# A multi-scale convolution on one core: weights first in both load queues, and GpSimd's ring sum added last for every image

## The reference, cut to what matters

```python
# x (8, 32, 64, 64); _gn normalises each of the 32 channels of each image over its 64x64 pixels
def _L0_conv_ref(x, w1, w3, w5, w_proj):
    xd = jnp.concatenate([x[:, :, 0::2, 0::2], x[:, :, 0::2, 1::2],
                          x[:, :, 1::2, 0::2], x[:, :, 1::2, 1::2]], axis=1)   # 128 channels, 32x32
    feats = jnp.concatenate([_dwconv(xd, w1, 1), _dwconv(xd, w3, 3), _dwconv(xd, w5, 5)], axis=1)
    y = jnp.einsum('bchw,oc->bohw', feats, w_proj[:, :, 0, 0])                 # 384 -> 128 channels
    ll, lh, hl, hh = jnp.split(y, 4, axis=1)
    ...                                                                        # interleaved back to 64x64
    return out
x = x + _L0_conv_ref(_gn(x), L0_conv_w1, L0_conv_w3, L0_conv_w5, L0_conv_w_proj)
```

## Time and profile before

| what | value |
|---|---|
| median of 3 runs | 148.43 us (147.65 to 148.79) |
| the profiled execution: its own time | 149.9 us |
| its span, first to last instruction | 148.1 us |
| busy in the span: PE / DVE / ACT / POOL | 131.2 / 132.1 / 105.0 / 111.2 us |
| mean granted TensorE clock | 0.987 |

### The profile page before, as it was taken

One profiled execution on the slowest core, in us unless ns is written; L12 is line 12 of the kernel. 1 busy time (PEld: TensorE's weight loads), 2 busy tenths in 40 slices (PEclk: granted clock), 3 DMA queues, 4 the chain that ended last, 5 costly groups with the idle time before them and its releaser, 6 DMA issues.

```text
span 148.1 us, 1521 instructions
## 1 busy us (share of the span) xinstructions
PE 131.2 (89%) x505; PEld 97.7 (66%) x505; DVE 132.1 (89%) x147; ACT 105.0 (71%) x107; POOL 111.2 (75%) x81
## 2 busy tenths in 40 slices
PE   5789999699399999999999929999999999999470
PEld 5677787487276687767776616777777777687130
DVE  7559959999799998999999999999999999999651
ACT  2069943999999999989995999999999150050000
POOL 6138659779999999999999898989999997039000
PEclk9999999999999999999999999999999999999959
DMA  4999999201600700700525899152399927778333
GB/s 129 241 227 203 209 209 212 47 4 31 120 2 0 150 2 4 150 0 0 110 40 104 179 193 206 39 113 38 71 212 178 206 50 142 146 165 187 72 67 75
DMA packets 35799, 16.78 MB, mean 113 GB/s; under 512 B 34000, under 2 KB 34128, under 8 KB 35408
## 3 DMA queue, kind: packets, MB, share of 16 engines
q1 hardware_dynamic: 32720, 9.18, 31.9%
q0 software_dynamic: 1440, 7.04, 24.4%
q10 hardware_dynamic: 1632, 0.48, 1.4%
HBM read 5.46 MB, written 4.19 MB: 65 GB/s over the span
## 4 chain that ended last, share of the span: by engine, by line
DVE 55%; POOL 16%; PE 12%; DMA 7%; issue 5%; ACTq 1%; DVEq 1%; POOLq 0%
DVE ACC L595 38%; POOL RING_SUM L314 14%; DVE ACC L592 8%; PE YP L668 6%; DVE F L609 4%; DMA w_sb<-in_L_conv_w_dram 4%; DMA LO<-G 3%; PE YP L732 3%; PE YP L719 2%; POOL rstd L285 1%; DVE ACC L587 1%; DVE dev L519 1%; DVE F L605 1%; DVE ACC L599 1%; POOL LO L303 1%
## 5 line engine op out<-in xcount | busy, mean ns | idle before, releaser
L314 POOL TENSOR_TENSOR RING_SUM<-RING_SUM,PROD 128x900 f32<-128x900 f32 (+1 forms) x41 | 86.9, 2119 | 7.2 <-ACT PROD L434 3.4
L595 DVE SCALAR_TENSOR_TENSOR ACC<-G,coef,ACC 128x930 f32<-128x930 f32 (+1 forms) x63 | 75.3, 1195 | 2.0
L434 ACT ACTIVATE PROD<-G,coef 128x900 f32<-128x900 f32 (+1 forms) x41 | 40.8, 1055 | 0.0
L668 PE MATMUL YP<-LO,whi 128*128 128x512 f32 (+1 forms) x144 | 38.2, 417 | 2.3 <-DMA LO<-G 2.3
L668 PE MATMUL YP<-HI,wlo 128*128 128x512 f32 (+1 forms) x144 | 37.5, 413 | 0.0
L668 PE MATMUL YP<-HI,whi 128*128 128x512 f32 (+1 forms) x144 | 36.4, 407 | 0.3 <-DVE nbias L526 0.3
L668 PEld LDWEIGHTS YP<-LO,whi 128*128 128x128 f32 x144 | 27.3, 190 | 11.1 <-DMA LO<-G 2.7
L668 PEld LDWEIGHTS YP<-HI,whi 128*128 128x128 f32 x144 | 27.7, 194 | 7.8 <-issue 0.8
L668 PEld LDWEIGHTS YP<-HI,wlo 128*128 128x128 f32 x144 | 27.3, 190 | 8.5 <-issue 1.9
L417 ACT ACTIVATE Y<-YP 64x1024 f32<-64x1024 f32 x14 | 15.3, 1095 | 14.3 <-PE YP L719 14.1
L396 ACT ACTIVATE G<-X,nbias,rstd 64x1024 f32<-64x1024 f32 x16 | 21.0, 1312 | 4.8 <-DVE nbias L507 4.5
(11 more groups left out here) (63 smaller groups left out, 74.7 us busy)
## 6 DMA issues: line engine op xcount, KB each, us to landing
X<-in_x_dram SPq DMA_DIRECT2D x16, 256.0 KB, 5.4
LO<-G POOLq DMA_DIRECT2D x7, 543.0 KB, 4.7
X<-Y POOLq DMA_DIRECT2D x3, 1024.0 KB, 7.0
out_dram<-X SPq DMA_DIRECT2D x12, 256.0 KB, 4.7
out_dram<-X SPq DMA_DIRECT2D x6, 128.0 KB, 2.4
XS<-in_x_dram SPq DMA_DIRECT2D x2, 256.0 KB, 3.2
XS<-in_x_dram SPq DMA_DIRECT2D x1, 512.0 KB, 7.7
out_dram<-X ACTq DMA_DIRECT2D x2, 128.0 KB, 2.6
```

What stands on the lines that cost most here:

```text
L314: pool.tensor_tensor(dst, dst, prod(b, k), ALU.add).then_inc(prod_added, 1)
L434: act.activation(prod(b, k), g_tap(b, POOL_OF[b][k + 1]), ACT.Copy, scale=of5(POOL_OF[b][k + 1])).then_inc(prod_ready, 1)
L595: dve.scalar_tensor_tensor(part(ACC, tap), g_tap(b, tap), of5(tap), part(ACC, tap), ALU.mult, ALU.add).then_inc(acc_step, 1)
L668: mm = nc.tensor.matmul(dst, w[:, n, :], src, start=start, stop=False, skip_group_check=True)
```

## The change: weights first, and the ring sum last

Eight things are changed together.

1. Loads: SP issues `w5` and `w3` ahead of the `XS` loads; ACT issues the projection weights first, then `w1`, then the two halves of image 0, which SP had.
2. `LATE` holds all eight images: each begins with the scaled copy L587 and ends with the addition of `RING_SUM`.
3. `POOL_N` is 5, 6, 6, 6, 7, 7, 7, 8: 44 products on POOL in place of 41, and 76 DVE taps in place of 79. Image 0 has one DVE tap more, images 4 to 7 one less.
4. POOL issues `low_image(b+1)` after the third product of image b, not after its last. The third `add_x` stands after product 6 of image 7, the last one; before, after product 4, the last but one.
5. PE: `ring(3)` and `ring(4)` move behind the `high` sets of images 5 and 6 (before: behind the high-image-by-low-weights sets of images 4 and 5). Warm-up matmuls are 7 + 2 + 2 on the identity and 8 of 512 columns (before 9 and 10). PE's sum of the statistics of image 1 comes three taps earlier, and PE waits in image 2 for the variance of the last pairs, not for their bias.
6. The scaling of `weff` 6 to 8 goes from POOL to ACT. POOL waits for all three `whi` before its first `wlo`, and makes the spread of image 1's statistics after the first `wlo`.
7. DVE: the small statistics instructions with two SBUF tensors are written as `tensor_scalar` with a scalar read per partition; a copy of the mean is added. DVE permutes the projection weights before its two `part_bn` of image 0.
8. POOL's third `inv_std` stands one product earlier, DVE's `variance(2)` one tap earlier.

```diff
-POOL_TAPS = [(0, 2), (-2, -2), (-2, 2), (2, -2), (2, 2), (-2, -1), (2, 1)]
-POOL_N = [6, 6, 6, 6, 6, 6, 6, 7]
+POOL_TAPS = [(0, 2), (-2, -2), (-2, 2), (2, -2), (2, 2), (-2, -1), (2, 1), (-1, -2)]
+POOL_N = [5, 6, 6, 6, 7, 7, 7, 8]
-LATE = (0, 1, 7)
-ADD_X_AT = [(4, 2), (6, 2), (7, 4)]
+LATE = tuple(range(8))
+ADD_X_AT = [(4, 2), (6, 2), (7, 6)]
-WARM = (9, 10)
+WARM = (7, 2, 2, 8)
-RING_AFTER_HIGH = {2: 0, 3: 1, 4: 2, 7: 6}
+RING_AFTER_HIGH = {2: 0, 3: 1, 4: 2, 5: 3, 6: 4, 7: 6}
-RING_AFTER_WLO = {4: 3, 5: 4, 6: 5}
+RING_AFTER_WLO = {6: 5}
-INV_STD_AT = {(0, 3): (3, 2, 3), (1, 2): (4, 3, COLS)}
+INV_STD_AT = {(0, 2): (3, 2, 3), (1, 2): (4, 3, COLS)}
         def _(sp):
+            sp.dma_start(w_sb[:, 0:W3_AT], w5.rearrange("c a h w -> c (a h w)")).then_inc(w_loaded, 16)
+            sp.dma_start(w_sb[:, W3_AT:W1_AT], w3.rearrange("c a h w -> c (a h w)")).then_inc(w_loaded, 16)
             load_parts(sp, 0, 0, 512, xs_loaded[0])
             load_parts(sp, 0, 512, 1024, xs_loaded[1])
-            load_image(sp, 0, image_loaded[0])
             load_parts(sp, 1, 0, 1024, xs_loaded[2])
...
                 for k in range(N_PROD[b]):
+                    if k == NEXT_IMAGE_AT and b + 1 < B:
+                        low_image(b + 1)
                     pool.wait_ge(prod_ready, products_before(b) + k + 1)
...
-            for n in range(ACT_SCALED, N_INNER):
-                pool.tensor_scalar(weff[:, n, :], wpT[:, 2, :], of5(INNER[n]), None, ALU.mult).then_inc(pool_scaled, 1)
+            pool.wait_ge(whi_ready, CHUNKS)
             for k in range(CHUNKS):
                 taps = slice(k * CHUNK, (k + 1) * CHUNK)
-                pool.wait_ge(whi_ready, k + 1)
...
-                dve.scalar_tensor_tensor(nbias[:, b:b + 1], agg1[:, b, 0:1], -1.0, rstd[:, b:b + 1],
-                                         ALU.mult, ALU.mult).then_inc(stats_ready, 1)
+                dve.tensor_scalar(nbias[:, b:b + 1], agg1[:, b, 0:1], rstd[:, b:b + 1], -1.0,
+                                  ALU.mult, ALU.mult).then_inc(stats_ready, 1)
...
-                dve.tensor_tensor(dev2[:, a:b], dev[:, a:b], dev[:, a:b], ALU.mult).then_inc(stat_step_in, 1)
+                for t in range(a, b):
+                    dve.tensor_scalar(dev2[:, t:t + 1], dev[:, t:t + 1], dev[:, t:t + 1], EPS,
+                                      ALU.mult, ALU.add).then_inc(dev2_ready, 1)
...
-                        if n == 2 * CHUNK:
+                        if n == CHUNK:
                             sum_parts(1)
```

More of the change, by code:

```diff
@@ L131, in build @@
         avg = sb("avg", [P, P], F32)
+        mean = sb("mean", [P, PAIRS], F32)
         mhalf = sb("mhalf", [P, COLS], F32)
@@ L327, in _ @@
             inv_std(1, 0, 1)
[L328 to L331 removed]
+            pool.wait_ge(whi_ready, CHUNKS)
             for k in range(CHUNKS):
                 taps = slice(k * CHUNK, (k + 1) * CHUNK)
[L334 removed]
                 pool.tensor_tensor(wlo[:, taps, :], weff[:, taps, :],
                                    whi[:, taps, :].bitcast(F32), ALU.subtract).then_inc(wlo_ready, 1)
[L338 to L340 removed]
+                if k == 0:
+                    pool.wait_ge(part_stats, 5)
+                    pool.tensor_tensor(spread[:, 1, :, :], stp[:, 1, None, :].to_broadcast([P, PARTS, STATS]),
+                                       mask[:, :, None].to_broadcast([P, PARTS, STATS]), ALU.mult).then_inc(spread_done, 1)
             low_image(0)
             inv_std(2, 1, 2)
[L343 to L345 removed]
+            for b in range(B):
                 sum_products(b)
@@ L516, in variance @@
                 dve.wait_ge(comb_done, n)
-                dve.tensor_tensor(dev[:, a:b], agg[:, a:b, 0], COMB[a][:, a:b, 0], ALU.subtract).then_inc(stat_step_in, 1)
-                dve.wait_ge(stat_step_in, 2 * n - 1)
-                dve.tensor_tensor(dev2[:, a:b], dev[:, a:b], dev[:, a:b], ALU.mult).then_inc(stat_step_in, 1)
-                dve.wait_ge(stat_step_in, 2 * n)
-                dve.scalar_tensor_tensor(vare[:, a + 1:b + 1], dev2[:, a:b], EPS, COMB[a][:, a:b, 1],
-                                         ALU.add, ALU.add).then_inc(stat_step, 1)
+                dve.tensor_copy(mean[:, a:b], COMB[a][:, a:b, 0]).then_inc(mean_copied, 1)
+                dve.tensor_tensor(dev[:, a:b], agg[:, a:b, 0], COMB[a][:, a:b, 0], ALU.subtract).then_inc(dev_ready, 1)
+                dve.wait_ge(dev_ready, n)
+                for t in range(a, b):
+                    dve.tensor_scalar(dev2[:, t:t + 1], dev[:, t:t + 1], dev[:, t:t + 1], EPS,
+                                      ALU.mult, ALU.add).then_inc(dev2_ready, 1)
+                dve.wait_ge(dev2_ready, b - 1)
+                dve.tensor_tensor(vare[:, a + 1:b + 1], dev2[:, a:b], COMB[a][:, a:b, 1], ALU.add).then_inc(stat_step, 1)
             def bias(n, a, b):
                 dve.wait_ge(rstd_done, n + 2)
-                dve.scalar_tensor_tensor(nbias[:, a + 1:b + 1], COMB[a][:, a:b, 0], -1.0, rstd[:, a + 1:b + 1],
-                                         ALU.mult, ALU.mult).then_inc(stats_ready, 1)
+                dve.wait_ge(mean_copied, n)
+                for t in range(a, b):
+                    dve.tensor_scalar(nbias[:, t + 1:t + 2], mean[:, t:t + 1], rstd[:, t + 1:t + 2], -1.0,
+                                      ALU.mult, ALU.mult).then_inc(stats_ready, 1)
             def add_w3(*taps):
                 for n in taps:
[L532 to L535, removed]
+                    dve.wait_ge(w5_scaled, n + 1)
                     dve.scalar_tensor_tensor(weff[:, n, :], wpT[:, 1, :], coef[:, w3_col(INNER[n]):w3_col(INNER[n]) + 1],
@@ L614, in _ @@
                        (0, 4): lambda: (variance(1, 1, 2), bn(2), aggregate(2)), (0, 5): lambda: bias(1, 1, 2),
-                       (0, 6): lambda: (bn(3), aggregate(3)), (0, 8): lambda: variance(2, 2, PAIRS),
+                       (0, 6): lambda: (bn(3), aggregate(3)), (0, 7): lambda: variance(2, 2, PAIRS),
                        (0, 9): lambda: bias(2, 2, PAIRS)}
@@ L724, in ring @@
                     mm.then_inc(conv_done, 1)
+            for _ in range(WARM[1]):
+                keep_warm(ident[:, :], P)
             pe.wait_ge(w_loaded, 48)
             nc.tensor.matmul(COEF_PS, ident_ph[:, :], w_sb[:, :], start=True, stop=True).then_inc(coef_ready, 1)
+            for _ in range(WARM[2]):
+                keep_warm(ident[:, :], P)
             sum_parts(0)
@@ L730, in _ @@
             zeros = LO[:, SLOTS - 1, :]
-            for _ in range(WARM[1]):
+            for _ in range(WARM[3]):
                 nc.tensor.matmul(YP[:, 0, 0:512], zeros[:, 0:P], zeros[:, 0:512], start=True, stop=True)
```

16 lines of the change are left out of this document (7 added, 9 removed).

## The result

The changed kernel takes 147.06 us (median of 20 runs, 145.29 to 148.65), the kernel before 148.55 (20 runs, 147.65 to 149.02). The ratio is 0.986, with a 95% interval of 0.984 to 0.988: 1.4% faster. The forecast was 142.8 with a range of 140.0 to 146.0, so the gain is a quarter of the one that was forecast, and the time lies above the range. The profiled execution took 148.02 with a span of 146.2, 1.0 above the median.

What follows compares the result with a forecast made beforehand. DVE bounded the kernel, PE close behind; after the change, the stores behind the third add_x: 129.0 + 1.1 + 11.5 + 0.9 = 142.5. Span falls 5.6, so 148.43 - 5.6 = 142.8 us, range 140.0 to 146.0.

Steps and rivals of the forecast that it cites:

- the part on the start: Kernel start: earlier weights, quicker weff additions and a shorter nbias give image 1's statistics at 20.8, not 24.66.
- its high halves start some 0.9 us earlier: ACT at the start: weights 1.2 us earlier, three more scalings cost 0.93, so high halves start some 0.9 us earlier.
- 1.2 less 0.93: Start: 1.2 us taken off by earlier weights (bounds 0 to 2); 0.93 us added by ACT's three more scalings.
- the largest term: Start: image 1's statistics ready at 20.8 and not 24.66, a gain of 3.9 us, bounded by 0 and 4.5.
- The rival on the start: The start gives little: no gain, 148.3 us, chance 0.1; half the gain, 145.5 us, chance 0.13.
- The rival on TensorE's clock: Fewer warm-ups leave PE's first real set at half clock, 3 us more, ring 4 holds ACT: 145 us, chance 0.05.
- The steps behind it: After the start: DVE's F of image 7 at 130.7, PE's last tap at 127.5, third add_x issued at about 122.
- the bound: Tail: third add_x lands at 129.0, then the last four images' stores, 2.10 MB in 11.5 us, end at 142.5.
- this step from span to median: End of the sum: the runs' median was taken to lie 1.5 us below the profiled time.
- the forecast's intermediate times: ACT's image 1 near 20.9, third X<-Y near 122, F of image 7 near 130.7.

Runs made afterwards that it cites:

- run 1: Changed kernel with image 0 loaded by SP's queue again, behind the two XS halves of image 0: 143.94 us, ratio to the kernel before 0.984.
- run 6: Kernel before with the loads in the changed kernel's order (w5, w3 first on SP; projection weights, w1, then image 0 on ACT): 150.40 us, ratio 1.014.
- run 4: Changed kernel with 20 warm-up matmuls of 512 columns in place of 8: 145.54 us, ratio to the kernel before 0.997.
- run 7: Changed kernel with nbias of images 0 and 1 again by scalar_tensor_tensor with two SBUF tensors: 147.93 us, ratio to the kernel before 0.991.
- run 10: Kernel of run 8 with nbias of images 0 and 1 again by scalar_tensor_tensor with two SBUF tensors: 140.74 us, ratio to the kernel before 0.947.
- run 2: Changed kernel with the third adding DMA behind product 4 of image 7, two products earlier: 144.81 us, ratio to the kernel before 0.994.
- run 11: Kernel of run 8 with the third adding DMA behind product 6 again: 144.26 us, ratio to the kernel before 0.963.
- run 8: Changed kernel with image 0 on SP's queue, the third adding DMA behind product 4, and 14 warm-up matmuls in place of 8: 139.68 us, ratio 0.940.

## Why the prediction was wrong, by its own steps

**The step that failed is in the part on the start**: "its high halves start some 0.9 us earlier". The step costed ACT's queue by its scalings and the weights by their place in the queue, and it never asked when image 0 would land once its load was moved. The move was in the list of the change, and the load kept its time of issue (1.64 before, 1.68 after), so I gave it no term. But image 0 landed at 11.90, where before it was there at 9.3. In run 1 its load, on SP's queue again, was issued almost 1 us later than here (2.60) and landed at 9.7, more than 2 us earlier. That the move made it late is shown (runs 1 and 6). How, is argued: SP, rid of it, issued `XS` of image 1 and then image 1 itself 0.5 to 2.5 us earlier, and the DMA engines, busy at 203 to 270 GB/s between 6 and 12 us, served these alongside. No run holds these loads back with image 0 on ACT's queue, so it could also lie in that queue itself, where 192 KB of projection weights stand ahead of it. ACT's high halves began at 11.97, 0.95 later than before, not 0.9 earlier.

Two sizes in the same step were wrong as well. By its own terms, 1.2 less 0.93, the halves should have started 0.3 us earlier and not 0.9. In run 1 they started 1.3 earlier (9.70 against 11.02), because the coefficients came earlier than the 1.2 us that I had taken (1.8 in the changed kernel, more in run 1); that its first real matmul (10.63) is near the forecast 11.2 is in part luck. And the warm-ups were taken at 0.44 us each and ran at 0.26. At the slower rate eight of them would have lasted until about 11.7 (8.21 + 8 x 0.44, an estimate), and PE would have waited for image 0 about 1.2 us and not 2.60.

**What hung on it was the largest term.** The statistics of image 1 were forecast at 20.8 with the remark that three engines have to agree; they came at 24.3 (24.32). PE's sum for them was to run at 18.0 and ran at 22.16, behind a set at half the clock. Of the 3.9 us, 0.3 arrived. The experiments divide the rest: half the late image, half the clock (runs 1 and 4). The rival on the start ("none" at 148.3, "half" at 145.5) is the case that came, and by its path it is "none": `X<-Y` was put at 127.5 there and stood at 126.60. Its span was to be 148.0; this 0.9 and a tail 0.8 shorter than forecast leave 146.3, and 146.2 was measured. Its cause was left open there, with a chance of 0.23 in all. The rival on TensorE's clock named the right mechanism at the wrong occasion: not a first set that the warm-ups hand over at the slower rate, but a gap behind them.

**The steps behind it were right in their durations.** They are shifted by the delay of the start:
- DVE's `weff` additions took 0.88 us for three without GpSimd beside them, as taken.
- A late image of ten taps is 13.68 us (43.66 to 57.34), forecast 13.66. DVE's path from `F` of image 0 (44.88) to that of image 7 (134.53) is 89.65 us, forecast 89.5. PE's image is 14.62 (42.85 to 57.47).
- GpSimd's image of five products takes 11.14 us (41.09 to 52.23), forecast 11.4. No product took over 2.30 us, and L584 with its output in PSUM took 1.286 to 1.290 us in all eight images, so neither engine held the other up. The rule of the Trainium skill (SBUF — State Buffer, Who interferes with whom) that `tensor_scalar` can lock GpSimd out doesn't act in this form. The other half of it, two SBUF inputs against GpSimd's reads, the trace of before and runs 7 and 10 bear out (1.60 to 1.92 us for one column).
- The tail is what was forecast, and the bound: the third `X<-Y` is followed by the last stores, 12.7 us from 133.5 to the end; forecast 13.5. From 135 to 145 the DMA moved 166 to 215 GB/s in every single microsecond, without a gap. 142.5 + 4.6 (the later `X<-Y`) - 0.8 = 146.3, measured 146.2. Runs 2 and 11 confirm it from both sides: the DMA two products earlier shortens the time, and two later lengthens it.
- One size at the end was wrong: the median lay 1.0 us under the profiled time and not 1.5. Of the miss of 4.3 us, 3.7 are thus the span (146.2 for 142.5) and 0.5 this step from span to median.

In run 1, which takes the late image away, the forecast's intermediate times hold to 0.7 us. So the mechanism was right but for one transfer, the first image's load in the first 12 us, and for the clock, which the gap before that image brought down.

## What to carry to other kernels

When a load moves to another queue, follow its landing and not only its issue, and what the old queue now issues earlier: here the issue kept its time, the landing came 2.6 us later, and the whole start waited for it. Keep TensorE busy until its real data is surely there; a gap of 2.6 us behind the warm-ups cost another 2.5 us in the set that followed, and cheap matmuls that filled the gap (twelve more in run 4, six more in run 8) removed that loss. And an edit's price belongs to the kernel in which it is measured: adding a slow engine's sum last gave 0.5% while the other engine was the bound, and 2.7% once the work had been shifted to the slow engine.

## What was not expected of the hardware

- The 512-column warm-ups ran at about 0.45 us each in the profile of before (ten in 4.61) and at 0.26 us in that of the changed kernel (eight in 2.09), both in stretches with a granted clock of 1.00 in the rows. Only the durations tell the rates apart there; no run explains the difference.
- After the fall, the clock stayed at 0.50 for six us (14 to 20) though PE worked nearly all that time from 14.6 on.
- One column of `scalar_tensor_tensor` with two SBUF tensors can take 1.60 to 1.92 us when GpSimd has a product of 2.0 us under way, and 0.16 when it has none. The 0.16 in the kernel before, at 10.58, stood beside a `tensor_scalar` of GpSimd that had begun at 10.55, so it isn't every GpSimd instruction that holds it up.
